# Second half of a two-layer kernel rearranged: fronts beside the last slots of the loop, one line of attention passes for both batches, one scaling chain for all eight tiles

## What is computed

```python
# layer 0
h = _layernorm(x) * (1 + ca) + sa
x = x + ga * chunked_linear_attention(h, 32 heads of 128)      # 16 groups of heads x 4 chunks = 64 slots
h = _layernorm(x) * (1 + cb) + sb
x = x + gb * (h @ (wscale * sign(weight) + wbias).T)           # "f"
# layer 1
h = _layernorm(x) * (1 + ca) + sa                              # "a"
q, k, v = h @ wq + bq, h @ wk + bk, h @ wv + bv                # 32 heads of 16, 8 kv heads
q, k = _rope(q), _rope(k)
x = x + ga * softmax(q k.T / 4) v
h = _layernorm(x) * (1 + cb) + sb                              # "h"
xn = h * rsqrt(mean(h * h) + eps)
H_res = sinkhorn(xn @ W_res.T + base, 50 rounds)               # a 4x4 matrix for every token
H_pre, H_post = softmax(xn @ W_pre.T + ..), softmax(xn @ W_post.T + ..)
y = (H_pre . h_streams) @ W_branch
x = x + gb * (((1 - g) I + g H_res) h_streams + y H_post)
```

## Time and profile before

| | |
|---|---|
| median of 3 runs | 1687.12 us (1684.72 to 1690.33) |
| profiled execution | 1688.87 us, span of the trace 1686.8 us |
| TensorE busy | 1340.1 us (79% of the span) |
| VectorE busy | 1113.9 us (66%) |
| GpSimd busy | 784.8 us (47%) |
| ScalarE busy | 641.0 us (38%) |
| mean granted TensorE clock | 0.852 of full |

### The profile page before, as it was taken

One profiled execution on the slowest core, in us unless ns is written; L12 is line 12 of the kernel. 1 busy time (PEld: TensorE's weight loads), 2 busy tenths in 40 slices (PEclk: granted clock), 3 DMA queues, 4 the chain that ended last, 5 costly groups with the idle time before them and its releaser, 6 DMA issues. The chain is left out here.

```text
span 1686.8 us, 19274 instructions
## 1 busy us (share of the span) xinstructions
PE 1340.1 (79%) x6160; PEld 922.1 (55%) x6160; DVE 1113.9 (66%) x2337; ACT 641.0 (38%) x1233; POOL 784.8 (47%) x721
## 2 busy tenths in 40 slices
PE   2768999999999999999999995687999669893000
PEld 0557767767767767777777673463333633322000
DVE  4644665566555666565566657797564977858998
ACT  0323433433333334344333331122555245654642
POOL 1336655755665756666566566560001600004144
PEclk8789999999999999999999997886777767775555
DMA  4121122122122121211221122300000000000001
GB/s 168 50 60 38 50 75 64 55 71 82 51 63 75 51 68 58 70 44 57 63 63 51 50 85 72 124 1 1 2 2 1 1 2 1 2 1 0 0 13 38
DMA packets 68019, 76.93 MB, mean 46 GB/s; under 512 B 5816, under 2 KB 39736, under 8 KB 67920
## 3 DMA queue, kind: packets, MB, share of 16 engines
q1 hardware_dynamic: 66048, 72.98, 14.2%
q10 hardware_dynamic: 1872, 2.72, 0.4%
HBM read 73.15 MB, written 2.28 MB: 45 GB/s over the span
## 5 line engine op out<-in xcount | busy, mean ns | idle before, releaser
L1094 DVE TENSOR_REDUCE nm<-banks 128x2 f32<-128x1024 f32 x128 | 153.4, 1216 | 45.7 <-PE banks L672 45.6
L1519 POOL TENSOR_TENSOR dec<-gb,gcol 128x512 f32<-128x512 f32 x64 | 70.8, 1106 | 210.2 <-DVE Sd L919 195.2
L1507 POOL TENSOR_TENSOR sw<-sw,sinT 128x512 f32<-128x512 f32 x80 | 103.0, 1287 | 140.7 <-ACT sw L1287 140.7
L1336 ACT ACTIVATE yTh<-yF 128x512 fp32r<-128x512 f32 x64 | 40.4, 632 | 330.3 <-DVE yF L953 330.3
L561 PE MATMUL banks<-st,qt 128*128 128x128 f32 x384 | 85.1, 307 | 61.3 <-DVE Sd L919 45.8
L891 DVE SCALAR_TENSOR_TENSOR gs<-tg,banks 128x512 f32<-128x512 f32 x64 | 44.0, 688 | 120.3 <-ACT tg L1294 120.3
L509 PE MATMUL banks<-hTh,wgh 128*128 128x512 f32 x256 | 122.2, 477 | 0.0
L693 PE MATMUL banks<-qsT,ksT 50*128 50x512 f32 x256 | 104.6, 579 | 7.9 <-ACT aqr L1396 5.7
L509 PE MATMUL banks<-hTh,wqh 128*128 128x512 f32 x256 | 107.3, 419 | 0.0
L561 PEld LDWEIGHTS banks<-st,qt 128*128 128x128 f32 x384 | 68.6, 216 | 70.9 <-DVE Sd L919 49.9
L589 PE MATMUL banks<-woh,yTh 128*128 128x512 f32 x256 | 104.7, 409 | 2.8 <-DVE yTl L956 2.8
(11 more groups left out here) (288 smaller groups left out, 3722.1 us busy)
## 6 DMA issues: line engine op xcount, KB each, us to landing
gb<-g_scr SPq DMA_DIRECT2D x64, 256.0 KB, 3.5
raw<-in_wmod SPq DMA_DIRECT2D x40, 256.0 KB, 2.7
raw<-in_wo SPq DMA_DIRECT2D x32, 256.0 KB, 2.8
raw<-in_wq SPq DMA_DIRECT2D x31, 256.0 KB, 2.7
raw<-in_wg SPq DMA_DIRECT2D x31, 256.0 KB, 2.7
mt<-mods_scr SPq DMA_DIRECT2D x20, 256.0 KB, 8.0
stg<-in_wmod SPq DMA_DIRECT2D x2, 1024.0 KB
xin<-in_x SPq DMA_DIRECT2D x8, 256.0 KB, 8.0
```

The source lines that it names most:

```text
L1094: ve.tensor_reduce(nm[:, i, p:32:16], pairs[z_][:, :].rearrange("p (g t) -> p g t", g=2), AX.X, ALU.max, negate=True).then_inc(*v_nm.up(b, ...
L1507: po.tensor_tensor(s_[:, :], s_[:, :], sinT[:, :], ALU.mult).then_inc(*g_rope.up("sin", kind, t, n))
L1519: po.tensor_tensor(dec[:, :, :], gb[s % 2][:, :, :], bc(gcol[:, t % 2, heads(t), n], 2, 128), ALU.subtract).then_inc(*g_dec.up("sub", s))
```

## The change

Everything after slot 59 is arranged anew; the first 59 slots keep their work and order.

- **Fronts.** `second_half` is gone. `first_front` (weights, residual, norm, turns and products of "f" for batch 0) is a stream of 26 steps: one in slot 60, eight in each of slots 61, 62 and 63, one behind the loop. `start_loads` is called at the start of slot 59 and not at its end, and also loads the attention weights. `second_front` does batch 1, merged with `starts` of batch 0.
- **Norm.** The normalised row is one ScalarE instruction (`norm`). The turn is now by block of channels (all four tiles at once), so the modulation is a column: it is applied while ScalarE drains the transposes, twice (once rounded, once into `hF`), and VectorE subtracts. The rows of "h" keep the modulation rows (`scaled_rows`). GpSimd has one more instruction for each tile's norm (`nmr`).
- **Bias and rotation.** The bias is one more product with two rows into the same bank. ScalarE copies q, k and v out, GpSimd makes two products, VectorE two products from the bank and one sum.
- **Passes.** Queries and keys of both batches are made first (`parts(0)` merged with `starts` of batch 1, then `parts(1)`), and `attentions` runs 16 quads in one line. `head(0)` is stepped in from the ninth quad on.
- **Scaling.** One chain over all eight tiles (128 values a partition), after `head(1)`, with `branch(1)` merged in. `finish` does all eight tiles behind it, VectorE with two of four streams (three in tiles 3 and 7).

```diff
@@ layer0_loop
+            beside = [0, 0, 0, 0] if s < NSLOT - 4 else [[0, 0, 0, 1], [2, 2, 2, 2], [2, 2, 2, 2], [2, 2, 2, 2]][s - NSLOT + 4]
+            if s == NSLOT - 5:
+                E.start_loads()
+                front = stream(E, first_front)
...
             E.outputs(s)
+            for _ in range(beside[0]):
+                front.step()
             E.norm_a(s)
...
             E.state(s)
+            for _ in range(beside[1]):
+                front.step()
             if s + 2 < NSLOT:
                 E.load_gb(s + 2)
...
-            if s >= NSLOT - 5:
-                second_half(E, s)
+            for _ in range(beside[3]):
+                front.step()
@@ Sync.start_loads
-            self.load_mod(0, 4, 0)
-            self.load_mod(0, 3, 0)
+            sp.wait_ge(*v_gate(15, 3))
+            self.load_cols()
+            self.load_mod(0, 5, 0)
             self.load_mod(0, 2, 1)
             for i in range(4, 8):
                 sp.dma_start(xin[i][:, :], x_in[i]).then_inc(*d_x[i].up("xin"))
-            for blk, b in ((4, 1), (3, 1), (5, 0), (5, 1)):
-                self.load_mod(0, blk, b)
+            self.load_mod(0, 5, 1)
+            sp.wait_ge(*v_yF(NSLOT - 5))
+            sp.dma_start(aqr[:, :, :], I["aq"].rearrange("(k p) n -> p k n", p=128)).then_inc(*d_a[0].up("aq"))
+            sp.dma_start(akr[:, :, :], I["akv"].rearrange("(k p) n -> p k n", p=128)).then_inc(*d_a[1].up("akv"))
@@ Scalar
+            ac.activation(hh[b][:, i % 4, :], acc[:, i, :], ACTF.Identity, bias=nmr[:, i:i + 1], scale=rs[:, i:i + 1]).then_inc(*a_n.up(of, i))
...
+            ac.activation(hT2h[b][:, k, :], banks[bk][:, :], ACTF.Identity, bias=s_, scale=c).then_inc(*a_hh.up("r", of, b, k))
+            a = ac.activation(hF[z_][:, :], banks[bk][:, :], ACTF.Identity, bias=s_, scale=c)
@@ Tensor.qkv
+            pe.matmul(banks[bq][:, :], one2[:, :], brow[:, 0:512], start=False, stop=True).then_inc(*p_qkv.up("q", i))
@@ streams
+    def first_front(E):
+        E.w_values()
+        yield
+        yield from weight_turns(E)
+        E.col_turn(E.bank())
+        yield
+        yield from residuals(E, "f", 0)
+        yield from norms(E, "f", 0)
+        yield from turns(E, "f", 0)
+        yield from ffns(E, 0)
...
-    def sinkhorn(E, b, t0, t1):
-        c, k = Sink(b, t0, t1), 0
+    def sinkhorn(E):
+        c, k = Sink, 0
...
-    def finish(E, b):
-        of = lambda i: (3 if i % 2 else 2) if b else 0
-        for i in range(4 * b, 4 * b + 4):
+    def finish(E):
+        of = lambda i: 3 if i % 4 == 3 else 2
+        for i in range(NT):
@@ story
-        fill, none = stream(E, starts, 1), Stream(iter(()), 0)
-        attention(E, 0, fill, none)
-        fill.rest()
-        pending = stream(E, behind)
-        attention(E, 1, none, pending)
-        merged(stream(E, head, 1), merged(taken(pending, 80), stream(E, branch, 0))).rest()
+        merged(stream(E, second_front), stream(E, starts, 0)).rest()
+        E.memsets(2)
+        merged(stream(E, parts, 0), stream(E, starts, 1)).rest()
+        stream(E, parts, 1).rest()
+        E.load_mods()
+        pending = joined(stream(E, head, 0), stream(E, mixes, 0))
+        attentions(E, pending)
+        pending.rest()
+        merged(stream(E, head, 1), stream(E, branch, 0)).rest()
         E.mix_y(1)
-        sk1 = merged(stream(E, sinkhorn, 1, 0, 2), stream(E, sinkhorn, 1, 2, 4))
-        merged(taken(sk1, 28), pending).rest()
-        merged(taken(sk1, 212), stream(E, branch, 1)).rest()
-        merged(sk1, stream(E, finish, 0)).rest()
-        stream(E, finish, 1).rest()
+        merged(stream(E, sinkhorn), stream(E, branch, 1)).rest()
+        stream(E, finish).rest()
```

More of the change, by code:

```diff
@@ L196, in build, with over @@
[L196 to L206, removed]
+    def over(kb, name, shape, dt=F32, end=None):
+        place[0] = base_h + int(kb * 1024)
+        t = sb(name, shape, dt)
+        assert end is None or place[0] <= base_h + end * 1024, name
+        return t
@@ L230, in build @@
[L230 to L234, removed]
-    nmp = sb("nmp", [128, 4, 2, 2, 2], F32R)
-    oS = sb("oS", [128, 512])
+    ksTs = [over(80, "ksT0", [128, 4, 512], F32R), over(56, "ksT1", [128, 4, 512], F32R)]
+    vps = [over(96, "vp0", [128, 4, 8, 32]), over(116, "vp1", [128, 4, 8, 32])]
@@ L248, in build @@
[L248 to L253, removed]
+    assert place[0] <= base_h + 130 * 1024
     d_scr = nc.dram_tensor("mods_scr", (4, 3072), F32, kind="Internal").ap()
@@ L1832, in norms @@
         i0 = 4 * b
-        for i in (i0, i0 + 1):
-            E.moments(of, i), (yield)
-        for i in range(i0, i0 + 4):
-            if i + 2 < i0 + 4:
-                E.moments(of, i + 2), (yield)
-            E.rows(of, i), (yield)
-    def turns(E, of, b, bks):
-        for j in range(4):
-            E.turn_h(of, 4 * b + j, bks[j % 2]), (yield)
+        for i in range(i0, i0 + 6):
+            if i < i0 + 4:
+                E.moments(of, i), (yield)
+            if i >= i0 + 2:
+                E.norm(of, i - 2), (yield)
@@ new lines, in second_front, with starts, parts @@
+    def second_front(E):
+        yield from residuals(E, "f", 1)
+        yield from norms(E, "f", 1)
+        yield from turns(E, "f", 1)
+        yield from ffns(E, 1)
+    def starts(E, b):
+        yield from norms(E, "a", b)
+        yield from turns(E, "a", b)
+    def parts(E, b):
+        i0 = 4 * b
+        for j in range(7):
+            if j >= 3:
+                for n in (4, 0, 1, 2, 3):
+                    E.turn_part(i0 + j - 3, n), (yield)
+            if 2 <= j < 6:
+                E.parts2(i0 + j - 2), (yield)
+            if j < 4:
+                E.qkv(i0 + j), (yield)
+            if 1 <= j < 5:
+                E.rope_add(i0 + j - 1), (yield)
+                E.parts1(i0 + j - 1), (yield)
@@ L1858, in pass_a_line @@
         for part in range(3):
[L1859 removed]
+            E.max_part(1, 7, part, E.spin() if part == 2 else None), (yield)
     def head(E, b):
         i0 = 4 * b
[L1863 to L1871 removed]
+        for j in range(7):
+            if j < 4:
+                E.residual("h", i0 + j), (yield)
+            if 1 <= j < 5:
+                E.moments("h", i0 + j - 1), (yield)
+            if 2 <= j < 6:
+                E.norm("h", i0 + j - 2), (yield)
+            if j >= 3:
+                E.scaled_rows(i0 + j - 3), (yield)
         for j in range(6):
@@ L2041, in layer0_loop @@
                 E.turn_v(t + 1)
+            for _ in range(beside[2]):
+                front.step()
             if ahead:
```

640 lines of the change are left out of this document (331 added, 309 removed).

## The result

The changed kernel takes 1747.41 us (median of 4 runs, 1739.40 to 1749.95) against 1686.34 us of the kernel before (4 runs): a ratio of 1.035, 95% interval 1.0312 to 1.0389. It is slower, as forecast, but by 61 us where 16 were forecast, and outside the range of 1681 to 1721. The profiled execution took 1747.37 us, with a span of 1744.5.

A forecast was written before the change was run, and what follows sets the result against it. It took TensorE to bound queries, keys and passes, VectorE the chain, handovers the four slots, VectorE and GpSimd the finish. Eight terms summed to +15.6 us on the median, 1702.7, given as 1703; range 1681 to 1721.

The forecast's parts named there:

- term 4: Queries and keys of both batches: TensorE's work at full clock, 64 us against 85.8, -21.8 us (-30 to -8).
- Term 1: Slot 60: the `gb` block of slot 61 lands behind all loads, at 1023, delaying slot 61; +15.1 us.
- Term 2: Slots 61 to 63, with batch 0's "f" front put in: 64.2 us against 52.8, +11.4 us (0 to 22).
- Term 3: Last `acc` to first `qkv` product: 44.5 us against 47.9, -3.4 us (-15 to +8).
- Term 5: Passes as one line of 16 quads, one start-up gained: 293.1 us against 312.0, -19.0 us (-25 to -8).
- rival C: Passes: a long line runs at a higher clock, nearer 0.8, quads some 2.1 us shorter; 1675 us, chance 0.08.
- Term 7: Chain with 128 values: 49 rounds of 2.16 us, 122.5 us in all against 101.9, +20.6 us.
- Term 8: Finish: all eight tiles exposed behind the chain, 43.8 us against 25.2, +18.6 us (+12 to +28).
- Term 6: Last `oS` to the start of batch 1's scaling: 36.5 us against 42.4, -5.9 us (-12 to 0).

The follow-up runs named there:

- four edits: Changed kernel with the order of parts as before, block of slot 61 ahead of the loads, gate later, two alternating chains of 64: 1692.03 us, ratio 1.0043.

## Why the prediction was wrong

The direction was right, the size was not. **The step that failed is term 4**, queries and keys: "TensorE's 27.6 us of work a batch", "at full clock, twice about 32 = 64". The work was sized right, 64.7 us. The waits were put at nothing, without a reason, though TensorE was idle for 6.9 of the 34.5 us of batch 0 before. The stage was not TensorE's: 27.4 us of waits and 16.1 us of lower clock come on top, with the 0.7 of work 44.2 in all. The step took a stage in which TensorE was busy most of the time before and assumed that it is all of the time now, though the change reorders `parts` and gives ScalarE copies of the queries that VectorE did. What would have shown it was at hand: the order of ScalarE's queue around `ksT`, and the shared bank, which the kernel before has too, and on which TensorE waited in batch 0, by the view of waits of the kernel before from 1119.5 to 1154.0:

```profile
PE banks L658 <- ACT ksT L1379: 3.1, 4, 0.8
```

Four waits of up to 0.8 us there became eight of up to 3.4. What the bank costs depends on how late its copy comes. The experiments show both: 10 to 15 us for the bank in three pairs of kernels, 17 to 18 for the order in two.

**Term 1** was right: 14.8 for 15.1, by the mechanism named (`dec` idle 17.9 us for the block), and undone by one move. The block landed some 4 us before the forecast's 1023, from loads that began 3.2 us earlier.
**Term 2** was low by 4.0: slots 61 and 62 took 34.2 for 32.8, slot 63 34.0 for 31.4. What it blamed, the order in slot 63, is not a cost of its own.
**Term 3** was low by 5.7; 4.3 of it is the wait for the gate's row, which the prediction did not look at.
**Term 5.** The start-up came out at 34.0 us, as forecast. In the profile of the changed kernel the rest is 11.9 us shorter than forecast. The clock in the passes was 0.77, above the 0.75 that the prediction named as a sign that it is wrong, and rival C's mechanism is there in part: two quads took 13.6 us each. The windows of the sixth and the seventh stretch from one `oS` to the next:

```profile
1377.94:1395.38 17.44, 16.44 (x74) 6.19 (x76) 10.25 (x13) 9.46 (x19) 0.00 (x0) 0.71 0.01 2
1395.38:1408.99 13.61, 12.35 (x74) 4.73 (x76) 10.24 (x13) 9.29 (x18) 0.00 (x0) 1.00 0.00 1
```

But eleven other kernels whose passes hold the same work took 283.0 to 296.7 us there, nine of them between 289 and 294 at 0.72 to 0.74, where the forecast was 293.1. Whether 281.2 is chance or usual for the changed kernel is open: its other three runs, of which there is no profile, took no longer (1739.40 to 1749.95). And where the sum fits, it does so by luck in part: with four edits the start-up was 37.5 us for 34, one quad beside `head(0)` 20.7, three more 17.9 to 19.0, and the last two, which have no maxima left, 11.9 and 11.5 where the sum had 17.25 and 14.2.
**Term 7** was high by 3.3: product 0.29, sum 0.29 or 0.37, reciprocal 0.35, a round 2.15 for the 2.16 forecast. So the 3.3 lie outside the rounds, which make 105.4 of the 119.2 us and leave 13.8 where the forecast had 16.5. Its product of 0.295 does not follow from its own doubling, which gives 0.31 (0.23 and twice 0.04); that would be 1.5 us more. For the product the rule of the Trainium skill ("VectorE: DVE Perf Modes", the section on the TRN2 errata) gives 291 ns at 128 values, and the trace agrees (0.29 us). The reciprocal is 353 ns by the groups of VectorE, where the same rule would make it 191 for its 32 values. The prediction's estimate by that rule, 291 ns for all six operations and a round of 1.95, would have been 10 us too little. The same section says that the latency between instructions is paid once a tile, which speaks for wide tiles. For a dependent chain wide was not faster here: two narrower chains in turn took 97.1 us where the wide one took 119.2. That alternative was in the profile before, as batch 1's rounds, and the prediction did not price it.
**Term 8** was low by 4.0, because VectorE's work was 43.0 us and not 37. What the sum missed is that VectorE is slower beside GpSimd. Two closes of the changed kernel, and what GpSimd did about the time:

```profile
1709.86 1.21 DVE L1232 TENSOR_TENSOR mx<-mx,mt 128x512 f32<-128x512 f32 x1
1715.94 0.68 DVE L1232 TENSOR_TENSOR mx<-mx,mt 128x512 f32<-128x512 f32 x1
```

```profile
1708.67 1.85 POOL L1686 TENSOR_TENSOR mx<-mx,prod 128x256 f32<-128x256 f32 x2
1711.14 1.30 POOL L1691 TENSOR_TENSOR acc<-acc,mx 128x512 f32<-128x512 f32 x1 [0.63 <-DVE mx L1232]
1712.41 2.67 POOL L1686 TENSOR_TENSOR mx<-mx,prod 128x128 f32<-128x128 f32 x4
1716.70 1.30 POOL L1691 TENSOR_TENSOR acc<-acc,mx 128x512 f32<-128x512 f32 x1 [1.62 <-DVE mx L1232]
```

The first close has a sum of GpSimd beside it and takes 1.21 us, the second has none and takes 0.68. The forecast took 0.65 for each; eight took 8.0 us. A mix takes 0.34 us alone and up to 1.35 beside such a sum.
**Term 6** was low by 2.9. The chain and the finish are 167.0 us long with one chain and 144.9 with two.

Where it went, then: of the 58 us, 22 are queries and keys, 15 the block of slot 61, 15 slots 61 to 63, 2 the stretch behind them, 17 the chain, 23 the finish, less 34 gained in the passes and behind them, and 3 in the part before slot 60. Undoing four orders and splitting the chain brings the change to the time before; none of the versions tried is faster than the kernel before by more than its interval.

## What to carry to other kernels

A stage's bound in the kernel before is no bound for the same stage reordered: for each engine that drains what the bound engine needs, read in its queue what now stands ahead of the drain, and whom that waits for. A PSUM bank given twice in a row turns each late drain into a stall (up to 3.4 us here). TensorE's idle time can cost more than itself: taking 16 us of waits out of queries and keys (27.4 to 11.4) gave back 32 us (108.2 to 76.0), because the granted clock rose from 0.8 to 1.00 at the same time. Before making a dependent chain of small vector operations wider, try it as two in turn (1.70 us a round here, for 2.15).

## What was not expected

- Twelve dependent VectorE operations of 64 values in two alternating chains took 1.70 us, six of 128 values 2.15 us, and six of 64 values alone 1.64 us: the second chain of 64 cost 0.06 us a round.
- TensorE's granted clock in the passes differs between quads of the same instructions: 13.6 us at 1.00, 15.9 at 0.79, 17.4 at 0.71. What decides it is open; it was not tried. It goes with up to 15 us in the passes between kernels, so gains of 4 us in another stage don't show in the time of four runs.
- A product of batch 1's chain in the kernel before (128x32, two inputs) took 0.19 us with GpSimd idle, and 0.48 on average, up to 1.30, with a GpSimd instruction beside it; its sums and reciprocals stayed at 0.19 and 0.20. In the timeline of VectorE, two products before and beside the GpSimd sums that start at 1598.53:

```profile
1598.36 0.31 DVE L1167 TENSOR_TENSOR T<-P,b 128x32 f32<-128x32 f32 x2
1600.36 0.99 DVE L1167 TENSOR_TENSOR T<-P,b 128x32 f32<-128x32 f32 x2
```

So batch 0's finish beside batch 1's chain was not free in the kernel before: a round of the two chains was 1.39 us without GpSimd's sums and often near 3 with them.
